# A three-layer graph network on one core: both groups of a lot in one PSUM bank, one-hot numbers spread four groups early, and two pieces of setup moved

## The reference

```
def _gnn_layer(nf, traj, src, dst, We, be, Wn, bn):
    ef = jnp.concatenate([nf[src], nf[dst], traj[:, None]], axis=-1)
    msg = jax.nn.leaky_relu(ef @ We.T + be, negative_slope=0.01)
    red = jax.ops.segment_sum(msg, dst, num_segments=nf.shape[0])
    h = jnp.concatenate([nf, red], axis=-1)
    return jax.nn.leaky_relu(h @ Wn.T + bn, negative_slope=0.01)
...
x = _layernorm(x + _L0_gnn_ref(x, L0_gnn_Wh, L0_gnn_weight, src, dst), axis=-1)
x = _layernorm(x + _L1_gnn_ref(x, edge_weight, src, dst, ...three layers' weights...), axis=-1)
```

## Time and profile before

| what | us |
|---|---|
| three runs | 11153.3, 11154.62, 11164.55 |
| the profiled execution, its own time | 11166.7 |
| its span, first to last instruction | 11165.6 |
| VectorE leaves the setup (first clear of the sort) | 46.64 |
| first one-hot of the first source phase, last | 2465.3, 3214.4 |
| rows of the layers' source phases: first matmul to last | 4786.3 to 5454.8, 6907.6 to 7578.6, 9029.8 to 9699.7 |

### The profile page before, as it was taken

How to read it: one execution, slowest core, us unless ns; L and a number is a source line. 1 busy time by engine, 2 the same in 40 slices (tenths; PEclk the granted TensorE clock), 3 DMA queues, 4 the chain that set the end, 5 groups by cost and what they waited for, 6 DMA issues and landing times. The chain is left out here.

```text
span 11165.6 us, 527753 instructions
## 1 busy us (share of the span) xinstructions
PE 8221.2 (74%) x180770; PEld 7196.5 (64%) x180770; DVE 9825.2 (88%) x22006; ACT 5658.0 (51%) x17855; POOL 5296.2 (47%) x5855
## 2 busy tenths in 40 slices
PE   7999997629976666599755557996555589855556
PEld 6999997317755556477655555775555577755554
DVE  6999998639989999777899997779999877799997
ACT  7888883117768887566422224663222266522222
POOL 0000001760027777433577773336777633477773
PEclk9999998559988887599999998999999999999997
DMA  1000000225556667667766665776666747766665
GB/s 42 8 8 9 8 8 9 49 49 216 216 185 195 192 197 190 98 215 250 229 197 197 197 187 113 250 250 207 196 197 197 162 161 250 247 196 197 197 197 98
DMA packets 1255832, 1748.34 MB, mean 157 GB/s; under 512 B 219360, under 2 KB 866418, under 8 KB 1254770
## 3 DMA queue, kind: packets, MB, share of 16 engines
q1 hardware_dynamic: 1009055, 1185.35, 32.6%
q0 software_dynamic: 245760, 549.71, 20.0%
q10 hardware_dynamic: 304, 4.93, 0.1%
HBM read 1049.39 MB, written 694.49 MB: 156 GB/s over the span
## 5 line engine op out<-in xcount | busy, mean ns | idle before, releaser
L1838 POOL DMA_INDIRECT work<-rows,quad_at x2928 | 3032.5, 1036 | 1032.4 <-issue 929.9
L1678 PE MATMUL bank<-work 128*128 128x64 bf16 x46848 | 1947.0, 199 | 1619.3 <-DVE work L1924 1616.8
L1678 PEld LDWEIGHTS bank<-work 128*128 128x128 fp8e4 (+1 forms) x46848 | 1748.1, 102 | 1762.5 <-issue 1693.8
L1863 ACT COPY work<-tabs 128x192 bf16 x2928 | 1029.1, 351 | 2976.3 <-PE bank L1879 2427.2
L1625 PE MATMUL bank<-work 128*128 128x64 bf16 x34560 | 1687.6, 193 | 3.0 <-issue 3.0
L1625 PEld LDWEIGHTS bank<-work 128*128 128x128 fp8e4 x34560 | 1448.7, 98 | 132.3 <-issue 4.4
L1642 DVE TENSOR_SCALAR work<-bank,part 128x512 fp8e4<-128x512 f32 x1440 | 1064.9, 751 | 492.1 <-PE bank L1603 491.7
L1879 PE MATMUL bank<-work 128*128 128x64 bf16 x35136 | 1296.3, 195 | 67.4 <-issue 34.6
L1912 DVE TENSOR_TENSOR work<-bank,work 128x512 f32<-128x512 f32 x1464 | 1090.6, 745 | 160.0 <-DMA work<-rows,quad_at 95.7
L1879 PEld LDWEIGHTS bank<-work 128*128 128x128 fp8e4 x35136 | 1155.8, 99 | 80.1 <-issue 50.9
L1709 POOL DMA_INDIRECT work<-rows,quad_at x976 | 995.6, 1020 | 421.0 <-PE bank L1678 225.2
(11 more groups left out here) (361 smaller groups left out, 18950.9 us busy)
## 6 DMA issues: line engine op xcount, KB each, us to landing
work<-hits_g SPq DMA_DIRECT2D x1464, 256.0 KB
rows<-work SPq DMA_DIRECT2D x1440, 256.0 KB, 2.5
hits_g<-work SPq DMA_DIRECT2D x976, 128.0 KB
rows<-work SPq DMA_DIRECT2D x480, 260.0 KB, 2.1
work<-hits_s SPq DMA_DIRECT2D x720, 128.0 KB, 2.1
work<-rows,quad_at POOLq DMA_INDIRECT x3904
hits_s<-work SPq DMA_DIRECT2D x240, 128.0 KB, 1.7
side<-meta POOLq DMA_DIRECT2D x720, 20.0 KB, 2.4
```

The costliest lines, as they stand in the source:

```text
L1678: last = ten.matmul(to[:, 0:D], hits_of(j), piece_of(j), start=j == 0 and k == 0, stop=j == QUAD - 1 and k == 2, skip_group_check=True)
L1838: pool.indirect_dma_start(quads[g // 2 % (GATHERED // 2)][:, half(g)], None, table, bass.IndirectOffsetOnAxis(ap=quad_at[:, g:g + 1], axis ...
L1863: sca.copy(window[q % 8].unsqueeze(1), tabs[:, 1, bass.ds(w, 1), :]).then_inc(s_window, 1)
```

## The change

Six edits.

1. In `source_phase` both groups of a lot go into one bank, `bank[4 + lot % 4]`, 256 columns each. The bank is read once, 512 columns: even lots by ScalarE, odd lots by VectorE, three lots behind (`BEHIND`).
2. The numbers of group g+4 are spread ahead of the rows of group g (`AHEAD`, before 2). The first two spreads stand ahead of the laps.
3. `hits` has 8 buffers of a lot instead of 4, and loaded one-hots come 5 lots ahead instead of 3.
4. SP stores three lots behind instead of two.
5. In `first_source_phase` VectorE clears `more`, not POOL.
6. The load of `x` moves from the setup to the sort block, behind the row loads of its first four blocks, and ScalarE's queue waits for `x` no more between the copies of the edges.

```diff
@@ setup
         nc.scalar.dma_start(dest, source.rearrange("(t p) -> t p", p=P)).then_inc(s_e, 16)
-        nc.scalar.wait_ge(*x_here)
...
-    nc.sync.dma_start(hr[:, 0:NW - 1, 0:D], x[0:full, :].rearrange("(w p) d -> p w d", p=P)).then_inc(s_x, 16)
-    nc.sync.wait_ge(*tail_zero)
-    nc.sync.dma_start(hr[0:TAIL, NW - 1, 0:D], x[full:N, :]).then_inc(s_x, 16)
@@ sort, SP
         for b in range(4):
             load(b)
+        syn.dma_start(hr[:, 0:NW - 1, 0:D], x[0:full, :].rearrange("(w p) d -> p w d", p=P)).then_inc(s_x, 16)
+        syn.wait_ge(*tail_zero)
+        syn.dma_start(hr[0:TAIL, NW - 1, 0:D], x[full:N, :]).then_inc(s_x, 16)
@@ first_source_phase
-        more_blank = po.did(nc.gpsimd.memset(more, 0.0))
+        more_blank = ve.did(nc.vector.memset(more, 0.0))
         nc.sync.wait_ge(*more_blank)
@@ source_phase
+        HITS = 8
+        AHEAD, BEHIND = 4, 3
...
+        def wait_read(engine, n, lap):
+            engine.wait_ge(s_read if n % 2 else s_read_too, past * (lots // 2) + lap * (MADE // 2) + (n // 2 + 1))
... SP
-                at_least(syn, s_rows, (l - 3) * GROUP_LOT, since)
+                at_least(syn, s_rows, (l - HITS + 1) * GROUP_LOT, since)
...
-                    load(l + 3, n + 3)
-                    store(l - 2, (n - 2) % MADE, lap - (n < 2))
+                    load(l + HITS - 3, n + HITS - 3)
+                    store(l - BEHIND, (n - BEHIND) % MADE, lap - (n < BEHIND))
... ScalarE
-                sca.copy(made_of(q), rows_of(q)).then_inc(s_read_too, 1)
+                sca.copy(made[n], row_bank[n % 4][:, :]).then_inc(s_read_too, 1)
...
+                if q % 4 == 3 and (not isinstance(g, int) or g // GROUP_LOT >= BEHIND):
+                    read(lap * MADE + (n - BEHIND), (n - BEHIND) % MADE, lap - (n < BEHIND))
... TensorE
-                to = row_bank[q % 4]
+                if q % GROUP_LOT == 0 and (not isinstance(g, int) or g >= 4 * GROUP_LOT):
+                    wait_read(ten, (n - 4) % MADE, lap - (n < 4))
+                to = row_bank[n % 4][:, q % GROUP_LOT * QUAD * D:(q % GROUP_LOT + 1) * QUAD * D]
...
-                if (not isinstance(g, int) or g + 2 < NS) and remade[(q + 2) % around]:
-                    spread(g + 2, (q + 2) % around, lap + (q >= around - 2))
+                if (not isinstance(g, int) or g + AHEAD < NS) and remade[q]:
+                    spread(g + AHEAD, (q + AHEAD) % around, lap + (q >= around - AHEAD))
                 rows(g, q, lap)
... VectorE
-                at_least(vec, s_rows, g - 7, since)
+                at_least(vec, s_rows, g - (HITS * GROUP_LOT - 1), since)
...
-                vec.tensor_copy(made_of(q), rows_of(q)).then_inc(s_read, 1)
+                vec.tensor_copy(made[n], row_bank[n % 4][:, :]).then_inc(s_read, 1)
...
+                if q % 4 == 1 and (not isinstance(g, int) or g // GROUP_LOT >= BEHIND):
+                    read(lap * MADE + (n - BEHIND), (n - BEHIND) % MADE, lap - (n < BEHIND))
```

More of the change, by code:

```diff
@@ L1481, in source_phase @@
         lots = NS // GROUP_LOT
-        since, since_hits, since_in, since_out = past * NS, past * NS // 2, past * (lots // 4) * 16, past * (lots // MADE) * 16
+        since, since_hits, since_in, since_out = past * NS, past * NS // 2, past * (lots // HITS) * 16, past * (lots // MADE) * 16
         room = Room(work, WORK - NG)
-        hits_home = [room.cut(GROUP_LOT * SLOTS // 4, BF16) for _ in range(4)]
+        hits_home = [room.cut(GROUP_LOT * SLOTS // 4, BF16) for _ in range(HITS)]
         hits = [home.bitcast(FP8).rearrange("p (g s) -> p g s", s=SLOTS) for home in hits_home]
         window = [room.cut(3 * D // 2, BF16) for _ in range(8)]
-        made = [room.cut(GROUP_LOT * QUAD * width).rearrange("p (g c) -> p g c", g=GROUP_LOT) for _ in range(MADE)]
+        made = [room.cut(GROUP_LOT * QUAD * width) for _ in range(MADE)]
         first_more = room.at
@@ L1543, in step @@
                     l = lap * MADE + n
-                    load(l + 3, n + 3)
-                    store(l - 2, (n - 2) % MADE, lap - (n < 2))
-            for l in range(3):
+                    load(l + HITS - 3, n + HITS - 3)
+                    store(l - BEHIND, (n - BEHIND) % MADE, lap - (n < BEHIND))
+            for l in range(HITS - 3):
                 load(l, l)
             laps(syn, NS, step, around)
-            for l in range(lots - 2, lots):
+            for l in range(lots - BEHIND, lots):
                 store(l, l % MADE, l // MADE)
@@ L1572, in _, with read @@
             next_windows = []
[L1574 to L1577, removed]
-                sca.copy(made_of(q), rows_of(q)).then_inc(s_read_too, 1)
+            def read(l, n, lap):
+                sca.wait_ge(s_rows, (l + 1) * GROUP_LOT + since)
+                at_least(sca, s_out[n], lap * 16, since_out)
+                settle(sca, "scalar", l)
+                sca.copy(made[n], row_bank[n % 4][:, :]).then_inc(s_read_too, 1)
             def step(g, q, lap):
@@ L1584, in step @@
                 sca.copy(window[q % 8].unsqueeze(1), tabs[:, 0, bass.ds(next_windows[q % 4], 1), :]).then_inc(s_window, 1)
-                if (not isinstance(g, int) or g >= 3) and by_scalar[(q - 3) % around]:
-                    read(g - 3, (q - 3) % around, lap - (q < 3))
+                n = q // GROUP_LOT
+                if q % 4 == 3 and (not isinstance(g, int) or g // GROUP_LOT >= BEHIND):
+                    read(lap * MADE + (n - BEHIND), (n - BEHIND) % MADE, lap - (n < BEHIND))
             laps(sca, NS, step, around)
-            for g in range(NS - 3, NS):
-                if by_scalar[g % around]:
-                    read(g, g % around, g // around)
+            read(lots - 2, (lots - 2) % MADE, (lots - 2) // MADE)
         @block.tensor
@@ L1652, in step @@
                     hit(g, q, lap)
-                if (not isinstance(g, int) or g >= 3) and not by_scalar[(q - 3) % around]:
-                    read(g - 3, (q - 3) % around, lap - (q < 3))
+                n = q // GROUP_LOT
+                if q % 4 == 1 and (not isinstance(g, int) or g // GROUP_LOT >= BEHIND):
+                    read(lap * MADE + (n - BEHIND), (n - BEHIND) % MADE, lap - (n < BEHIND))
             laps(vec, NS, step, around)
-            for g in range(NS - 3, NS):
-                if not by_scalar[g % around]:
-                    read(g, g % around, g // around)
+            for l in (lots - 3, lots - 1):
+                read(l, l % MADE, l // MADE)
         block.__exit__(None, None, None)
```

46 lines of the change are left out of this document (15 added, 31 removed).

## The result

The changed kernel takes 10724.0 us (median of 4 runs, 10717.17 to 10729.64) against 11159.48 us (4 runs, 11153.3 to 11164.55): a ratio of 0.961, 95% interval 0.9593 to 0.9626. That is 435 us less. The forecast was 10746 us, worked out as 409 us less than the profiled execution of before.

A forecast was written before the change was run, and what follows sets the result against it. Bound: TensorE and VectorE late to each other in the layers' source phases, plus waits ahead of the first and in setup. 260 + 134 + 15 = 409 off 11166.7 gives 10758, 12 less against the median: 10746 us; range 10640 to 10870.

The forecast's parts named there:

- That is latency, not throughput: Layers' source phases: TensorE waits for VectorE's compares, VectorE for TensorE's spreads (93.0 us out of 400); neither engine is full.
- The source phases, 260 forecast: Layers' three source phases: earlier spreads remove the 0.33 us wait a period; laps of 9.72 us, 87 us gained each.
- the loop closings stay: Layers' source phases: each closing of the loop still costs TensorE 0.6 us a lap, since nothing makes it rarer.
- the loop's closing was the compares too: Rival, layers' source phases: the closing's gap goes too, gain 369 us instead of 260, total 10637 us; chance 0.12.
- The reads: Layers' source phases: one 512-column read for two of 256; VectorE 8.2 to 8.4, ScalarE 8.3 us a lap; cost zero.
- the rival with ScalarE at the pace: Rival, layers' source phases: ScalarE's lap reaches 10.7 us, gain 84 instead of 260; chance 0.16 together with VectorE and DMA.
- Loads and stores: Layers' source phases: loads 5 lots ahead, stores 3 behind; same bytes, DMA share 0.85, below 1, so cost zero.
- The clear, 134 forecast: Ahead of the first source phase: VectorE's clear (2.1 us) avoids POOL's 99 scatters, 134 us gained; scatters beside it cost 0 to 12.
- The setup, 15 forecast: Setup: with ScalarE's queue not waiting for `x`, the sort starts at 31 instead of 46.56; 15 us gained, range 12 to 20.
- if the rows land at 20: Setup: rows of `dst` for the test of the order land at 20 us (between 15 and 23.2), so the sort starts at 31.
- The sentence on the turns between queue rows: Setup: DMA engines alternate queue rows by packet; if `dst` landed only with the last copy, sort at some 37, gain 9 us.
- the rival of a slower kernel: Rival, source phases: TensorE is granted a lower clock; at mean 0.80 the whole gain of 409 us is gone; chance 0.02.

## Why the prediction was right, and where it was off

**The view.** "That is latency, not throughput" held. The early spreads alone move no work from one engine to another and remove none, yet they give 285 of the 436 us that the whole change is worth in that batch; taking them back costs 276. The engines' sums of work had room for it, as worked out.

**The source phases, 260 forecast, 297 measured.** The plain period was forecast at 2.28 us and is 2.30. The term that was mis-sized is "the loop closings stay": 0.6 us a lap were carried over, and 0.19 remain. That alone is 25 us a phase (60 x 0.41), of which the 0.02 a period takes back 5, and single delays that the sum of regular laps leaves out some 7. The rival "the loop's closing was the compares too" named the right cause and gave it 0.12, though not all of it goes. Four kernels order it: spreads two groups early with 256-column banks 0.6, two early with a bank for a lot 0.35, four early 0.19 to 0.23 with either. A reading that fits, and that no run shows by itself: a delay of TensorE at the closing also starts the next compare later while the compare is what it waits for, and with four groups of lead only the closing's own part is left. How the 0.6 of before splits between closing and compares was not measured. 60 laps of 9.39 make 563 us; the measured 570 holds some 7 us more, a part of which is traced in the last section.

**The reads.** VectorE's read of 512 columns takes 0.68 us and ScalarE's 0.59; the prediction had 0.69 to 0.74, and 0.58. Neither engine released TensorE in the stretch from 4750 to 5150, and the rival with ScalarE at the pace did not come. Edits 1, 3 and 4 together were worth 7 us a phase with late spreads (670 to 663) and 4 to 5 with early ones (575 to 571).

**Loads and stores.** The DMA share went to 0.89 instead of 0.85, and the landing of a store from 2.6 to 3.2 us (median). That is dearer than forecast, yet TensorE waited for a load only 1.8 us out of 400 there.

```profile
rows<-work SPq DMA_DIRECT2D x339, 256.0 KB, 3.2
```

**The clear, 134 forecast, 137 measured.** Every step of it stands in the timeline. VectorE's clear took 1.76 us instead of 2.1, and the scatters cost nothing beside the phase; the allowance of up to 12 us was not needed.

**The setup, 15 forecast, 6.4 measured.** The step that failed is "if the rows land at 20". The range allowed 15 to 23.2 and they landed at 28.90, later than before, so the 6.4 us lie outside the 12 to 20 given for this term. The 23.2 came from a row in which only one copy ran beside the load, and no row stood behind the 20 and the 15. The sentence on the turns between queue rows, by which the rows land only with the last copy and the term is 9 us, was the nearer one: the last copy, issued at 3.46, took 24.8 us to land. What neither saw is that the load by itself kept only 0.2 to 0.4 of the DMA engines busy. The test of the order, 9.7 us behind it, was right to 0.1. TensorE's first spread came at 2321.34 instead of about 2315, which is these 9 us less the 3 of the clear.

**No change of clock.** The stretches at 99% busy have a granted clock of 1.00, so the rival of a slower kernel, which needed a lower one there, did not come.

**Errors that offset.** The two profiled executions are 445 us apart where 409 were forecast. Of these 36 us the source phases are +37, the clear +3, the setup -9, and +5 are in the rest (0.2 + 13.2 - 8.7). That last part is luck of the execution, since one stretch of it alone varies by up to 24 us between the thirteen profiles. The setup's shortfall hid a quarter of what the source phases gave beyond the forecast.

## What to carry to other kernels

When two engines wait for each other and neither is full, count first how many groups the producer is ahead of the consumer. Here two more groups of lead, in buffers that were there already, did two thirds of a change of six edits. Look at what stands in the queue ahead of a small step that everyone waits for, and give the step to an engine that is idle by then. And when a transfer is to run beside fewer others, check that it can use the room: the load in 125 rows could not.

## What the hardware showed besides

- In the layers' source phases POOL's queue pauses at fixed places. In the kernel with `x` in the setup, a load of lines came after 3.74 us of idling instead of the 0.2 to 0.8 around it, and TensorE then waited 1.02 us for it:

```profile
4954.15 0.55 POOL L1546 DMA_DIRECT2D side<-meta  x1 [3.74 <-PE bank L1609]
...
4957.05 0.39 PE L1589 MATMUL bank<-side,first_row 128*128 128x512 bf16 x1 [1.02 <-DMA side<-meta]
```

  The changed kernel has the same pauses:

```profile
4782.22 0.55 POOL L1545 DMA_DIRECT2D side<-meta  x1 [3.56 <-PE bank L1608]
...
4925.20 0.55 POOL L1545 DMA_DIRECT2D side<-meta  x1 [3.74 <-PE bank L1608]
...
5068.83 0.55 POOL L1545 DMA_DIRECT2D side<-meta  x1 [3.32 <-PE bank L1608]
```

  Between two of them lie 121 loads, and each of the three phases has three pauses after the same numbers of loads. The kernel before has them after the same numbers too, where they are 169 us apart (at 4960.23, 5128.81 and 5297.48, of 4.30, 3.68 and 3.76 us). So they go by the count of POOL's loads and not by time. Behind the pause at 4954.15 the next loads followed after only 0.2 us of idling each. Their buffers had been free for a while, so the row matmul that the bracket names is not what held them up. TensorE's waits for lines, with the sum in us, the times and the longest, out of 4750 to 5150, come one behind each pause:

```profile
PE bank L1588 <- DMA side<-meta: 1.8, 3, 1.3
```

  They are 1.8 of the some 7 us between 563 and 570. What makes POOL pause was not tried.
- Three copies of 1562.5 KB within DRAM, issued one behind the other, landed after 11.3, 14.9 and 24.8 us beside the load of `dst` in 125 rows, and after 7.8, 12.3 and 15.9 us without it. That load moved as much data as each of them and cost the last copy 9 us.
